# A two-block transformer kernel on one core: gate and up weights kept by blocks of 128 output rows, one turning instruction for each piece, and two buffers for the pieces' codes

## What is computed

```python
x = x + tanh(g_xattn[1]) * cross_attention(layernorm(x), ctx, 16 heads)
x = x + tanh(g_ffn[1])   * ffn(layernorm(x))

def nvfp4_linear(x, w, s_in):              # every 16 neighbours share a scale
    s_w = 448 * 6 / max(abs(w))
    xq = fake_quant_nvfp4(x, s_in)         # values 0, 0.5, 1, 1.5, 2, 3, 4, 6 times the scale
    wq = fake_quant_nvfp4(w, s_w)
    return einsum("bsh,oh->bso", xq, wq)

def ffn(x):                                # gate_w, up_w: (2048, 512); down_w: (512, 2048)
    gate_out = nvfp4_linear(x, gate_w, s_in)
    up_out   = nvfp4_linear(x, up_w, s_in)
    return nvfp4_linear(silu(gate_out) * up_out, down_w, s_in_down)
```

## Time and profile before

| | |
|---|---|
| median of 3 runs | 1780.79 us |
| profiled execution | 1780.83 us, span 1779.0 us |
| mean granted TensorE clock | 0.902 of 2.4 GHz |
| busy share of the span | TensorE 76%, VectorE 79%, ScalarE 39%, GpSimd 14% |
| share of the chain that ended last | VectorE 45%, TensorE 33%, ScalarE 8%, DMA 4%, SyncE's queue 2% |

### The profile page before, as it was taken

The page is one execution under the profiler, slowest core; times in us unless marked ns, Lnnn a source line. Parts: engine busy times, 40 slices in busy tenths (PEclk is TensorE's granted clock), DMA queues, the critical chain, the costliest instruction groups (busy, mean ns, idle before and its releaser), DMA issues.

```text
span 1779.0 us, 22434 instructions
## 1 busy us (share of the span) xinstructions
PE 1356.1 (76%) x8120; PEld 695.2 (39%) x8120; DVE 1409.3 (79%) x2440; ACT 692.7 (39%) x2106; POOL 243.1 (14%) x197
## 2 busy tenths in 40 slices
PE   5043737889787988698878978798879887997775
PEld 4021314434363435343443435343534354343421
DVE  6988886877887787878887788779787888786786
ACT  2113205542374326442554236432734164414420
POOL 1102200031002200131003100320023001310000
PEclk9556867999899999999999989999999999999987
DMA  9165862043202410053104320342013300521002
GB/s 349 70 236 136 191 171 47 1 71 60 71 2 43 87 50 25 8 88 83 25 1 78 53 71 2 60 72 57 16 30 66 83 25 7 89 45 40 7 18 59
DMA packets 267428, 119.69 MB, mean 67 GB/s; under 512 B 244122, under 2 KB 244634, under 8 KB 265782
## 3 DMA queue, kind: packets, MB, share of 16 engines
q1 hardware_dynamic: 267318, 118.27, 28.5%
HBM read 49.04 MB, written 8.39 MB: 32 GB/s over the span
## 4 chain that ended last, share of the span: by engine, by line
DVE 45%; PE 33%; ACT 8%; issue 6%; DMA 4%; SPq 2%; POOL 0%; DVEq 0%; ACTq 0%
PE bank L1109 25%; PE bank L1196 6%; ACT region L545 4%; DVE amax L835 4%; DVE hid L840 3%; DVE pair L844 3%; DVE stats L696 2%; DMA hqt<-pair 2%; DVE region L935 2%; DVE th L877 2%; DVE pair L859 2%; DVE region L727 2%; DVE pair L852 2%; DVE sr L810 2%; SPq L302 1%
## 5 line engine op out<-in xcount | busy, mean ns | idle before, releaser
L1196 PE MATMUL bank<-w_dn,region 128*128 128x512 fp8e4 x1024 | 243.7, 386 | 41.6 <-DMA region<-region 41.6
L1109 PE MATMUL bank<-w_up,xt 128*128 128x512 fp8e4 x1024 | 247.6, 389 | 31.3 <-ACT region L503 16.6
L1109 PE MATMUL bank<-w_gate,xqt 128*128 128x512 bf16 x512 | 146.8, 414 | 99.4 <-DVE th L877 56.3
L430 POOL TENSOR_TENSOR region<-g,region 128x512 f16<-128x512 f32 x128 | 178.2, 1396 | 297.5 <-ACT region L503 289.8
L545 ACT ACTIVATE region<-bank,nm 128x77 f32<-128x77 f32 x512 | 161.0, 353 | 66.8 <-DVE nm L930 66.8
L512 ACT ACTIVATE th<-bank,each 128x512 f32<-128x512 f32 x112 | 77.0, 687 | 271.7 <-PE bank L1109 271.7
L877 DVE SCALAR_TENSOR_TENSOR th<-th,bank 128x512 f32<-128x512 f32 x112 | 76.8, 686 | 129.5 <-ACT th L512 129.5
L500 ACT ACTIVATE g<-bank 128x512 f32<-128x512 f32 x128 | 76.4, 597 | 246.9 <-PE bank L1109 188.4
L1196 PEld LDWEIGHTS bank<-w_dn,region 128*128 128x128 f16 x1024 | 101.5, 99 | 167.5 <-DMA region<-region 43.1
L1109 PE MATMUL bank<-w_down,hqt 128*128 128x512 bf16 x496 | 132.2, 427 | 43.8 <-DMA hqt<-pair 43.8
L1109 PEld LDWEIGHTS bank<-w_up,xt 128*128 128x128 f16 x1024 | 101.6, 100 | 162.2 <-ACT region L503 20.5
(11 more groups left out here) (208 smaller groups left out, 2468.5 us busy)
## 6 DMA issues: line engine op xcount, KB each, us to landing
xin<-in_x SPq DMA_DIRECT2D x16, 512.0 KB, 4.6
out_x<-x SPq DMA_DIRECT2D x16, 512.0 KB, 2.9
region<-in_w_up_t SPq DMA_DIRECT2D x1, 4096.0 KB, 13.7
hid<-in_gate_w SPq DMA_DIRECT2D x4, 1024.0 KB, 5.3
x<-in_gate_w SPq DMA_DIRECT2D x4, 1024.0 KB, 6.1
hid<-in_up_w SPq DMA_DIRECT2D x4, 1024.0 KB, 5.3
x<-in_up_w SPq DMA_DIRECT2D x4, 1024.0 KB, 5.7
hid<-in_down_w SPq DMA_DIRECT2D x4, 1024.0 KB, 4.8
```

Source lines behind the costliest of these rows:

```text
L430: eng.tensor_tensor(hn[1][:, t % 2, ns], g32[:, s % 2, :], hn[0][:, t % 2, ns], ALU.subtract).then_inc(sg["hl"], 1)
L1109: last = mm(out, lhs, rhs, start=(n == 0), stop=(n == len(pairs) - 1))
L1196: last = mm(bank[2 + t % 2][:, :], ht[i][:, t % 2, f, :], w_dn[:, f, :], start=(f == 0 and i == 0), stop=(f == KF - 1 and i == 1))
```

## The change

`w_gate` and `w_gup` become `[P, KF, D]`: block of 128 output rows, then input chunk, then the 128 rows of the block. The 4 blocks of a piece now lie side by side in the destination in the order in which they lie in the source, and the piece is turned by one transposing transfer of 128 x 2048. The matmuls of `gate_up` read their 512 values as 4 runs of 128 that lie 512 values (1024 bytes) apart. The codes of even pieces still go to `hq`, those of odd pieces to `xqt`, which is free until then; the one semaphore `wt_done` is split into `wt_even` and `wt_odd`, and L859 of piece `m` waits for `turn(m-2)`. Nothing else differs, and no computed value does.

```diff
-WT_AT = [16 * (TILES * min(m, 2 * PIECES) + max(m - 2 * PIECES, 0)) for m in range(len(FP4_PIECES) + 1)]
-WT_DONE = WT_AT[-1]
...
-        w_gate = sb("w_gate", [P, KD, F], BF16)
-        w_gup = sb("w_gup", [P, KD, F], BF16)
+        w_gate = sb("w_gate", [P, KF, D], BF16)
+        w_gup = sb("w_gup", [P, KF, D], BF16)
...
+        xqt_all = xqt[:, :, :, :].rearrange("p t k c -> p (t k c)")
...
+        piece_codes = (hq[:, :], xqt_all)
...
                 sp.wait_ge(sm["piece_codes"], m + 1)
+                done = ("wt_even", "wt_odd")[m % 2]
                 if n == 2:
-                    sp.dma_start_transpose(w_down[:, :, i * P:(i + 1) * P], hq[:, :]).then_inc(sm["wt_done"], 16)
+                    sp.dma_start_transpose(w_down[:, :, i * P:(i + 1) * P], piece_codes[m % 2]).then_inc(sm[done], 16)
                 else:
-                    for t in range(TILES):
-                        c = TILES * i + t
-                        sp.dma_start_transpose((w_gate, w_gup)[n][:, :, c * P:(c + 1) * P],
-                                               hq[:, t * D:(t + 1) * D]).then_inc(sm["wt_done"], 16)
+                    sp.dma_start_transpose((w_gate, w_gup)[n][:, TILES * i:TILES * (i + 1), :]
+                                           .rearrange("p c (k j) -> p (c k) j", j=P),
+                                           piece_codes[m % 2]).then_inc(sm[done], 16)
...
-                code, hq_ = code_all[:, fs], hq[:, fs]
+                code, hq_ = code_all[:, fs], (hq if piece is None else piece_codes[piece % 2])[:, fs]
...
-                if q == QUANT_PARTS - 1 and m:
-                    dve.wait_ge(sm["wt_done"], WT_AT[m])
+                if q == QUANT_PARTS - 1 and m >= 2:
+                    dve.wait_ge(sm[("wt_even", "wt_odd")[m % 2]], 16 * (m // 2))
...
-                    last = product(bank[4 + i][:, :], [(xqt[:, t, k, :], w[:, k, ns]) for k in range(KD)])
+                    last = product(bank[4 + i][:, :].rearrange("p (c j) -> p c j", j=P),
+                                   [(xqt[:, t, k, :], w[:, 4 * n:4 * n + 4, k * P:(k + 1) * P]) for k in range(KD)])
```

More of the change, by code:

```diff
@@ L205, in build @@
                  "loaded_o loaded_up loaded_dn loaded_piece0 loaded_piece1 split wout_hi wout_lo ctx_psum ctx_done tern_part tern_done wsum_all "
-                 "wmax_part wmax_all piece_read piece_codes wt_done last_turn0 last_turn1 tanh_done").split()
+                 "wmax_part wmax_all piece_read piece_codes wt_even wt_odd last_turn0 last_turn1 tanh_done").split()
         per = dict(xin=32, var1=1, var2=1, var3=1, var4=2, rstd1=1, rstd2=1, rstd3=1, rstd4=2,
@@ L1056, in _ @@
             dve.wait_ge(sm["piece_read"], len(FP4_PIECES))
-            dve.wait_ge(sm["wt_done"], WT_DONE)
+            for turned in ("wt_even", "wt_odd"):
+                dve.wait_ge(sm[turned], 16 * len(FP4_PIECES) // 2)
             for g in range(GROUPS - 2):
@@ L1202, in gate_up @@
                 t, n = divmod(u, 4)
-                ns = slice(n * D, (n + 1) * D)
                 for i, (w, read) in enumerate(((w_gate, "hg"), (w_gup, "hid"))):
@@ L1314, in _ @@
             pe.wait_ge(sm["piece_codes"], len(FP4_PIECES))
-            pe.wait_ge(sm["wt_done"], WT_DONE)
+            for turned in ("wt_even", "wt_odd"):
+                pe.wait_ge(sm[turned], 16 * len(FP4_PIECES) // 2)
             for g in range(GROUPS - 2):
```

## The result

The changed kernel took 1765.81 us (median of 4 runs, 1763.84 to 1768.03) against 1780.6 us; the ratio is 0.9924, interval 0.991 to 0.9939. It was timed once more later, on another occasion, beside new runs of the kernel before: 1768.05 us (5 runs, 1766.45 to 1769.23) against 1781.0, ratio 0.9929, interval 0.9915 to 0.9943. So it is 13 to 15 us faster, where 12.1 us were forecast.

The account below looks back on a forecast made before the run. VectorE was taken to bound the first phase B, held up by waits for turns. 1780.8 - 13.6 (waits) + 1.5 (GpSimd stretching) + 0 (seams) = 1768.7 us, stated as 1768.5; range 1763 to 1776, about 80%.

Parts of the forecast that it names:

- What bounds the stretch: First phase B: VectorE sets its length, held up 13.6 us by L859's waits for turns; savings come off nearly one for one.
- Two code buffers: VectorE's L859 in first phase B: waiting for turn(m-2) instead of turn(m-1) removes all 13.6 us of waits.
- The tight load (piece 7): SyncE's queue: load goes out about 8.5 us after L859 of piece 4, leaving 1.4 to 3.6 us of room.
- One transfer for four: SyncE's queue: 2.3 us per turn instead of 5.22, L503 released near 175 us; same waits removed, nothing added.
- the third rival: First phase B: transfers become the bound, DMA engines full, VectorE gets a wait back; 1771 to 1776 us, chance 14%.
- GpSimd's stretching: First phase B: VectorE instructions beginning during GpSimd ones last longer, 4 to 7 us instead of 4.2; 1.5 us taken as lost.
- The seams: TensorE's 1024 gate_up matmuls: reading 4 runs of 128 instead of one of 512 costs nothing.
- The rival: Seams cost on TensorE in later rounds: 4.6 ns each gives 1783 us, 11.7 ns gives 1805; chance 9%.

Follow-up runs that it names:

- the second profile: The changed kernel run again unchanged, on another occasion, beside new runs of the kernel before: 1768.05 us, ratio 0.9929.
- the early rows: Changed kernel with the next group's rows (load_x(1)) issued ahead of the last two turns instead of behind them: 1761.13 us, ratio 0.9906 to the kernel before.

## Why the prediction was right

*What bounds the stretch.* Right. VectorE's time is the length of the first `phase_b`; 13.8 us given back as work bring back 13.9 us of median time against the first timing and 11.7 us against the second.

*Two code buffers.* Right: all five waits vanished, and the buffers alone give the whole gain. The tight load (piece 7) held: it was issued at 204.16, 8.3 us after L859 of piece 4 at 195.86, where I had put 8.5.

*One transfer for four.* Right that the two parts take away the same waits. Wrong in what it frees: I took 2.3 us on the queue for each turn from the rows of down, of which none stands behind a `turn_ht`; five of the eight turns of gate and up took 3.0 to 5.5 us. L503 was released at 176.36 and not near 175, and the third rival's full engines are real. It cost nothing, since nobody on the path waits there. My argument against that rival misread the rows: the fullest stretch, 178 to 188 us, is mostly VectorE's 5.73 us wait for a turn (180.24 to 185.97), and the block scales begin only at 188.15. What kept the rival away is the second buffer: piece 2's turn, issued at 175.04, was needed at 195.86 and not at 177.69, and with one buffer alone a wait of 4.84 us stood there. Of the five waits that I expected to shrink by 2.2 us each with this part alone, the three shorter ones went whole, one shrank by 2.6 us, and the long one by only 0.9. The Trainium skill's DMA: Bandwidth & Descriptors, section Rules for kernel authors, advises to coalesce many small transfers into a large one; here that was worth 8 us of waiting with one buffer and nothing measurable with two.

*GpSimd's stretching.* I took 1.5 us, and the sum came out, but in part by luck. The stretched instructions from piece 0's L859 on sum to 6.7 us in the changed kernel and 5.2 us before by the same count (a row's duration less the usual one of its kind), so 1.5 us. Yet 0.8 us of that lies at 157 to 162 us, ahead of the first wait that the change takes away; the nine GpSimd instructions that I had walked through cost 0.7 us more than before (0.9 us in the second profile). In their place stand two things that I had not seen: the 0.6 us wait for GpSimd's root, which L859's wait had hidden, and 0.4 us of the usual short gaps between instructions, which the waits had swallowed. 13.6 - 1.5 - 0.6 - 0.4 = 11.1 us against the 11.2 us measured; in the second profile 13.6 - 0.8 - 0.6 - 0.4 = 11.8. My sum had 12.1.

*The seams.* Right, at nothing. The rival falls: the layout alone is no slower. The sentence of the Trainium skill, Advanced Engine Details and Errata, section PSUM Cachelines, on non-contiguous patterns, if it is read for the moving operand, does not hold for runs of 128, 16 or, but for 5%, 4 values; it does for runs of 2 and 1. Read for the product in PSUM, no run here tests it.

*What missed.* The median gained 14.8 us, or 13.0 us in the second timing, the profiled execution 16.7 us. The part above 11.2 to 11.8 us is none of my terms: it lies in the later rounds, which differ by 6 us between two executions of one program, and the granted clock is the difference where I looked. In every kernel with a shortened stretch the median gained more than the stretch did (11.0 against 7.8 us for the single transfer, 13.6 against 12.1 for the buffers, 18.5 against 16.8 for the early rows), so a part may belong to the change; how much, and how much is chance, stays open.

## What to carry to other kernels

A wait of a producer for its only output buffer is worth nearly its full length when the producer sets the stage (11.2 to 11.8 of 13.6 us here), and a second buffer that lies idle at that time takes it away for nothing. Making the transfer faster is a weaker means to the same end, and where the queue and the DMA engines are full it hardly shortens a wait (5.73 to 4.84 us here). After such a gain, read the last wait of the stage again: moving one load ahead of two unrelated transfers was worth another 5 us.

## What the runs showed of the hardware that I had not expected

TensorE reads a moving operand of 2-byte values in runs that lie 1024 bytes apart without any cost down to runs of 16, with 5% more at runs of 4, twice the time at runs of 2 and four times at single values, some 1.7 ns for each run of up to 4 values. For single values the spacing was 3.43 to 3.46 us for 4 matmuls both in a stretch with a mean grant of 0.91 and in one of 0.75:

```profile
979.40:986.20 6.80, 6.80 (x9) 0.91 (x8) 0.69 (x1) 0.69 (x1) 0.36 (x1) 0.91 0.99 125
...
1025.60:1032.50 6.90, 6.90 (x9) 0.98 (x8) 0.69 (x1) 0.69 (x1) 0.00 (x0) 0.75 0.00 0
```

So that limit does not follow TensorE's clock. A SyncE transposing transfer of 128 x 2048 that takes 1.8 us of the queue alone took up to 5.5 us of it directly behind others, with the DMA engines full; two turns of down in the kernel before were issued with full engines too (shares of 1.05 and 1.07) and took only 2.7 and 2.8 us, so full engines alone do not make the 5.5 us.
